# Waits at the two ends of an attention stage, and the work around them

## The reference

```python
x = x + tanh(g_xattn[0]) * attention(layernorm(x), ctx, ctx, mask)    # scores of all 16 heads, softmax, V, W_o
y = layernorm(x)
logits = einsum('bsd,ed->bse', y, gate_w); affinity = softmax(logits)
gating, idx = top_k(transpose(affinity), 56)                          # 56 rows of a batch for each expert
h = silu(y[idx] @ w_gate) * (y[idx] @ w_up)
x = x + tanh(g_ffn[0]) * scatter_add(idx, gating * (h @ w_down))
```

## Time and profile before

| | |
|---|---|
| median of three runs | 1863.48 us (1860.78 to 1865.54) |
| the profiled execution | 1861.66 us, its span 1859.8 us |
| TensorE busy in the span | 1738.0 us (93%), mean granted clock 0.974 |
| DVE, ScalarE, GpSimd busy | 1044.9, 840.6 and 204.0 us |
| attention stage, first scores to barrier | from 301 to 871 us |
| expert stage, first product to end | from 892 us |

### The profile page before, as it was taken

How to read it: one execution, slowest core, us unless ns; L and a number is a source line. 1 busy time by engine, 2 the same in 40 slices (tenths; PEclk the granted TensorE clock), 3 DMA queues, 4 the chain that set the end, 5 groups by cost and what they waited for, 6 DMA issues and landing times.

```text
span 1859.8 us, 28459 instructions
## 1 busy us (share of the span) xinstructions
PE 1738.0 (93%) x10502; PEld 1542.7 (83%) x10502; DVE 1044.9 (56%) x1801; ACT 840.6 (45%) x1483; POOL 204.0 (11%) x287
## 2 busy tenths in 40 slices
PE   7999993999999999993899999999999999999995
PEld 6998992778777777761899999999999999999995
DVE  6666662878877877854453544535445354353541
ACT  3232321878777777860443433434334344343430
POOL 0000010202211220201000201102001020020101
PEclk9999996999999999996899999999999999999998
DMA  6545446467567656613333533434335353353421
GB/s 235 219 177 195 175 156 186 124 141 185 139 139 178 159 134 157 158 54 103 115 107 108 142 114 112 138 105 141 113 100 152 103 141 112 102 151 104 121 101 20
DMA packets 76190, 251.90 MB, mean 135 GB/s; under 512 B 10785, under 2 KB 10785, under 8 KB 74817
## 3 DMA queue, kind: packets, MB, share of 16 engines
q1 hardware_dynamic: 63968, 215.88, 37.9%
q0 software_dynamic: 12128, 34.80, 8.1%
HBM read 188.01 MB, written 51.61 MB: 129 GB/s over the span
## 4 chain that ended last, share of the span: by engine, by line
PE 51%; POOL 1%; DMA 0%; DVE 0%; issue 0%; DVEq 0%; ACT 0%; POOLq 0%
PE gu_ps L1579 11%; PE gu_ps L1577 11%; PE gu_ps L1578 11%; PE y_ps L1594 6%; PE y_ps L1596 5%; PE y_ps L1595 5%; PE y_ps L1605 1%; PE gu_ps L1563 1%; DMA xg<-xn_rows,gather_i 0%; POOL out L1437 0%; POOL xg L1427 0%; DVE xs_lo L1512 0%; DVE y_cols L1539 0%; PE gu_ps L1623 0%; DVE y_sb L1517 0%
## 5 line engine op out<-in xcount | busy, mean ns | idle before, releaser
L1577 PE MATMUL gu_ps<-xs_hi,ws_hi 128*128 128x448 f32 x1024 | 371.7, 363 | 3.0 <-DVE xs_lo L1512 3.0
L1579 PE MATMUL gu_ps<-xs_hi,ws_lo 128*128 128x448 f32 x1024 | 371.8, 363 | 0.0
L1578 PE MATMUL gu_ps<-xs_lo,ws_hi 128*128 128x448 f32 x1024 | 370.5, 362 | 0.0
L1507 DVE TENSOR_TENSOR ws_lo<-w_raw,ws_hi 128x1024 fp32r<-128x1024 f32 x192 | 235.3, 1226 | 188.9 <-ACT ws_hi L1457 188.5
L1457 ACT ACTIVATE ws_hi<-w_raw 128x1024 fp32r<-128x1024 f32 x192 | 201.7, 1051 | 164.1 <-PE y_ps L1596 146.6
L1254 PEld LDWEIGHTS t_ps<-cst,sm 112*125 112x125 f32 x1536 | 204.3, 190 | 85.2 <-issue 32.4
L1254 PE MATMUL t_ps<-cst,sm 112*125 112x112 f32 x1536 | 234.0, 281 | 31.0 <-DVE e_t L978 14.3
L863 ACT ACTIVATE sm<-sm,least 112x752 f32<-112x752 f32 x256 | 234.4, 917 | 27.7 <-DMA v_rows<-v_out 16.8
L970 DVE CUSTOM_DVE_ANT_0 sm<-m_ps,mq 112x752 f32<-112x752 f32 x256 | 229.8, 935 | 29.8 <-PE m_ps L1238 28.1
L1577 PEld LDWEIGHTS gu_ps<-xs_hi,ws_hi 128*128 128x128 f32 x1024 | 192.3, 188 | 15.2 <-issue 3.3
L1578 PEld LDWEIGHTS gu_ps<-xs_lo,ws_hi 128*128 128x128 f32 x1024 | 192.3, 188 | 14.0
(11 more groups left out here) (146 smaller groups left out, 2408.4 us busy)
## 6 DMA issues: line engine op xcount, KB each, us to landing
w_raw<-wstream SPq DMA_DIRECT2D x192, 512.0 KB, 3.5
ks<-k_split SPq DMA_DIRECT2D x192, 188.0 KB, 5.4
k_split<-k_split SPq DMA_DIRECT2D x32, 752.0 KB, 3.4
v_rows<-v_out SPq DMA_DIRECT2D x16, 750.0 KB
vs<-v_rows SPq DMA_DIRECT2D x16, 750.0 KB
c_raw<-ctxT SPq DMA_DIRECT2D x7, 1500.0 KB, 12.8
qs<-q_hi POOLq DMA_DIRECT2D x64, 112.0 KB, 5.3
mq_raw<-maskq SPq DMA_DIRECT2D x7, 656.2 KB, 10.1
```

The source lines that it names most:

```text
L1507: nc.vector.tensor_tensor(w_lo[s][:], w_raw[s][:], w_hi[s][:], ALU.subtract).then_inc(wlo_done[s], 1)
L1577: nc.tensor.matmul(o, w_hi[s][:, w], xs_hi[:, c], start=(c == 0), stop=False)
L1578: nc.tensor.matmul(o, w_hi[s][:, w], xs_lo[:, c], start=False, stop=False)
L1579: mm = nc.tensor.matmul(o, w_lo[s][:, w], xs_hi[:, c], start=False, stop=(c == DC - 1))
```

## The change

It has four parts.

1. The mask of batch 0 is loaded by SyncE among the first loads, straight into mq, and masked in place by DVE after the norm of batch 0, early in the first stage; mq_first, GpSimd's waits for qs and its load are gone. In the attention stage SyncE waits only for the first store of each half of V before it loads V of batch 0. wo and gatew are loaded in turn 6 of batch 0, and TensorE waits for them where it first uses them. The eight tiles e_t are numbered anew, so that the three that overlay nothing (FREE_TILES) serve heads 0 to 2; ScalarE and DVE wait for all stores in turn 3 (early_stores), SyncE in turn 8.
2. x2_out goes from DVE's turn 10 to GpSimd's turn 12, ahead of the output store, which moved there from turn 9.
3. In the last batch the output projection is made in pieces (project_last) in m_ps[0] and m_ps[1], the score accumulators: two of the four quads after turns 14 and 15, the third before the last values, the fourth after. The turns of x2 (turn_last) take each half of the rows as soon as it is normed and go to w_ps and m_ps[1], copied by ScalarE and DVE. DVE's affinity of batch 6 stands before the last normalise.
4. w_raw lies where the keys of the attention stage lie, and SyncE loads the first four weight units in attend's end, once the last scores are made.

```diff
+            with ExitStack() as late:
+                sb(late, "below", [P, IC * SLOTS - E_OVER * (KC // 2) * PAIR])
+                w_raw = [sb(late, f"w_raw{j}", [P, UNIT]) for j in range(NRAW)]
             ks = sb(mid, "ks", [3 * WAYS, KSLOTS, SK], F32R)
-            with ExitStack() as early:
-                mq_first = sb(early, "mq_first", [QP, QC, S2], I32)
...
                 load_x(0)
+                sp.dma_start(mq[:, :, 0:S2].bitcast(I32), maskq[0:1].rearrange("o p c n -> p (o c) n")).then_inc(mq0_in, 16)
                 pair(0, False)
...
                                        part[g * DK:g * DK + DK].bitcast(F32)).then_inc(qs_in[g], 16)
-                for g in range(NG):
-                    hold(qs_in[g], 48)
-                pool.dma_start(both.mq_first[:], maskq[0:1].rearrange("o p c n -> p (o c) n")).then_inc(mq0_in, 16)
...
-                    nc.vector.tensor_scalar(mq[:, :, 0:S2], both.mq_first[:], 0, MASKED, ALU.is_equal, ALU.mult).then_inc(mq_done, 1)
+                    nc.vector.tensor_scalar(mq[:, :, 0:S2], mq[:, :, 0:S2].bitcast(I32), 0, MASKED, ALU.is_equal, ALU.mult).then_inc(mq_done, 1)
...
                 norm(0)
+                mask_queries()
                 with dve.Fori(1, B // 2 - 1) as i:
...
-        e_t = both.e_t + [sb(st, f"e_t{j}", [KP, KC // 2, PAIR]) for j in range(E_OVER, 2 * HG)]
+        e_t = [sb(st, f"e_t{j}", [KP, KC // 2, PAIR]) for j in range(E_OVER, 2 * HG)] + both.e_t
...
                 def start():
                     for k in range(KC // VT):
-                        hold(v_stored[k], 16 * B)
+                        hold(v_stored[k], 16)
                     load_v(0, 0)
-                    sp.dma_start(wo_sb[:], wo).then_inc(att_in, 16)
-                    sp.dma_start(gw_sb[:], gatew).then_inc(att_in, 16)
-                    for k in range(2):
-                        hold(k_stored[k], 16 * B * NG // 2)
...
+                        if t == 6 and first:
+                            sp.dma_start(wo_sb[:], wo).then_inc(att_in, 16)
+                            sp.dma_start(gw_sb[:], gatew).then_inc(att_in, 16)
+                        if t == 8 and first:
+                            for k in range(KC // VT):
+                                hold(v_stored[k], 16 * B)
+                            for k in range(2):
+                                hold(k_stored[k], 16 * B * NG // 2)
...

                 def end():
                     load_res(B - 1)
+                    hold(m_made, NS * B)
+                    for u in range(NRAW):
+                        sp.dma_start(w_raw[u][:], wstream[u]).then_inc(w_in[u], 16)
                     sp.wait_ge(x_in, 16 * (B + 1))
...
+                def x2_out(b, j):
+                    flag = flags_sb[:, j]
+                    hold(rest_free, R_USES * b + R_Y + 3)
+                    hold(flag_step, 5 * b + 5)
+                    hold(out_stored, 16 * b)
+                    for c in range(QC):
+                        nc.gpsimd.tensor_scalar(x2o[:, c], x2[:, c], flag[:, 3, c:c + 1], None, ALU.add).then_inc(x2o_done, 1)

                 def spread_parts(b, q):
...
+                            if t == 12:
+                                x2_out(b - 1, 1 - j)
                                 store_out(b - 1)
                         if not last:
...
-                def start():
+                def early_stores():
                     for k in range(KC // VT):
                         act.wait_ge(v_stored[k], 16 * B)
                     for k in range(2):
                         act.wait_ge(k_stored[k], 16 * B * NG // 2)
+
+                def start():
                     for h in range(XLEAD):
                         for qc in range(QC):
...
+                        if first and t == FREE_TILES:
+                            early_stores()
...
                     copy_parts(B - 1, NG - 1)
-                    for n in range(2):
-                        x2_columns(B - 1, n)
+                    x2_columns(B - 1, 0)
...
-                def x2_out(b, j):
+                def flags(b, j):
+
                     flag = flags_sb[:, j]
-                    dve.wait_ge(rest_free, R_USES * b + R_Y + 3)
-                    after(dve, out_stored, 16 * b)
-                    for c in range(QC):
-                        nc.vector.tensor_scalar(x2o[:, c], x2[:, c], flag[:, 3, c:c + 1], None, ALU.add).then_inc(x2o_done, 1)
-
-                def flags(b, j):
-
-                    flag = flags_sb[:, j]
+                    after(dve, x2o_done, QC * (b - 1))
                     for qc in range(QC):
                         dve.wait_ge(masked[qc], H * b + KSLOTS + 1)
...
-                def residual(b, c):
+                def residual(b, c, src):
...
-                            if t == 10:
-                                x2_out(b - 1, 1 - j)
                             if t == 15:
...
-                    for q in (NG - 2, NG - 1):
-                        normalise(b, q)
+                    normalise(b, NG - 2)
                     affinity(b - 1, (b - 1) % 2)
-                    residual(b, 0)
-                    residual(b, 1)
+                    normalise(b, NG - 1)
+                    for c in range(QC):
+                        residual(b, c, m_ps[c][0:QP, 0, :])
                     dve.wait_ge(rest_free, R_USES * b + R_Y + 3)
                     dve.nop(nofuse=True)
                     moments(b, 1, x2)
                     norm_2(b)
-                    x2_out(b, b % 2)
+                    dve.wait_ge(rest_made, R_USES * b + R_XNT + 2)
+                    nc.vector.tensor_copy(xT[:, 1], m_ps[1][:, 1, 0:2 * S]).then_inc(rest_free, 1)
...
+                            pe.wait_ge(att_in, 32)
...
+
+                def project_last(qc, quads):
+
+                    b = B - 1
+                    if quads[0] == 0:
+                        pe.wait_ge(masked[qc], H * B)
+                        pe.wait_ge(att_in, 32)
+                    pe.wait_ge(cx_done, NG * b + quads[-1] + 1)
+                    for q in quads:
+                        mm = nc.tensor.matmul(m_ps[qc][0:QP, 0, :], cx[:, q, qc * QP:qc * QP + QP], wo_sb[:, q, :],
+                                              start=(q == 0), stop=(q == NG - 1))
+                    if quads[-1] == NG - 1:
+                        mm.then_inc(rest_made, 1)
+
+                def turn_last():
+
+                    b = B - 1
+                    pe.wait_ge(rest_free, R_USES * b + R_XNT + 1)
+                    for qc in range(QC):
+                        pe.wait_ge(xn2_done, QC * b + qc + 1)
+                        for c in range(DC):
+                            a = c % 2 * S + qc * QP
+                            o = m_ps[1][:, 1, :] if c // 2 else w_ps
+                            mm = nc.tensor.transpose(o[:, a:a + QP], xn2[:, qc, c * P:c * P + P], ident[0:QP, 0:QP])
+                            if qc == QC - 1 and c % 2:
+                                mm.then_inc(rest_made, 1)

...
-                    pe.wait_ge(att_in, 32)
...
+                        if last and t >= H - QC:
+                            project_last(t - (H - QC), (0, 1))

                 def end():
                     b = B - 1
                     turn_parts(b, NG - 1)
+                    for qc in range(QC):
+                        project_last(qc, (2,))
                     for part in range(HG - 1):
                         values(b, NG - 1, part)
                     for qc in range(QC):
-                        for k in range(2):
-                            project_out(b, qc, k, True)
-                    for n in range(2):
-                        turn_x2(b, n)
+                        project_last(qc, (3,))
+                    turn_last()
                     logits(b)
                     turn_affinity()
...
-                for u in range(NU):
+                for u in range(NRAW, NU):
                     load(0, u)
```

29 lines of the change are left out of this document (16 added, 13 removed).

## The result

The changed kernel took **1838.74 us** in the median of four runs (1836.25 to 1839.79), the kernel before 1863.55 on the same chip (four runs, 1860.78 to 1865.54): a ratio of 0.9865, 95% interval 0.9853 to 0.9877, 24.8 us faster. Forecast were 42.0 us and a range of 1815 to 1834. The direction was right, the size was not: the time lies 4.7 us above the range.

A forecast was written before the change was run, and what follows sets the result against it. TensorE was taken to bound the kernel, gains lying only where it stands still: 29.0 + 4.6 + 3.4 + 1.5 + 3.5 = 42.0 us off 1861.7 gives 1819.7, as a median 1821.5; range 1815 to 1834.

The forecast's parts named there:

- Nothing in the change shortens a matmul, so all it can give lies where TensorE stands still: Whole kernel: gains only at the two seams of the attention stage and some tenths in each batch.
- Each is met by 0 to 5 us. I cost it at 0: First batch: stores at turn 3, V at turn 5 and K of head 8 arrive in time; cost 0.
- The rival of the late transfer: First batch: V, K of head 8 or the stores late, 3 to 11.5 us, typically 6, so 1827.5; chance 0.24.
- The first batch, 29.0 us: Seam from projections to first batch: waits for mask and gate weights go and the clock stays up; 29.0 us.
- I take it that 2.4 GHz stays: First seam: with scores after 1.5 us of silence the clock does not fall; 29.0 us in place of 26.2.
- the rival's 26.2: First seam: the clock falls all the same, 26.2 us in place of 29.0, so 1824.3; chance 0.18.
- x2_out, 4.6 us: Batches 1 to 7: x2_out leaves DVE's turn 10, saving 0.66 us a batch, seven times; 4.6 us.
- Both together are under 0.83, so both go: Steady batch: TensorE's waits of 0.47 and 0.19 us vanish as DVE loses 0.83 us of work.
- The lower bound of the term: Batches 1 to 7: x2_out's move gains 0 if ScalarE's copies take over.
- The gather, 3.5 us: First experts: gathers land 4.0 us after issue, with fewer weight loads beside them; 3.5 us, bounds 1.7 and 4.3.
- The splits can start with the stage: First experts: four weight loads done early, so splits start with the stage and three reloads meet the gather.
- The last batch, 3.4 and 1.5 us: Last batch: output projection in pieces gains 3.4 us; turns of x2 by halves bring the logits 1.5 us earlier.

The follow-up runs named there:

- 3: Changed kernel, but DVE waits before its first split of weights until GpSimd has copied the first expert's gather indices; 1840.29 us.
- 16: The kernel before with part 1 of the change alone, the moved waits and loads of the first batch; 1841.10 us.
- experiment 8: Changed kernel with three more transposes of a constant behind each of the first six scores, to keep TensorE busier; 1839.58 us.
- 10: Changed kernel, but DVE's first splits of the expert stage wait until the four gathers have landed; 1836.64 us.
- Experiment 9: Changed kernel with expert-stage tiles reordered: h_hi back at byte 99072, split weights moved, w_raw left where the change put it; 1831.32 us.
- experiment 1: Changed kernel with 64 bytes put ahead of h_hi and w_raw and 64 more ahead of xg, h_hi at byte 19968; 1849.28 us.
- experiment 6: Changed kernel, DVE's first splits to wait until the four gathers are issued, SyncE's loads of units 4 and on until they have landed; 1839.18 us.
- 5: Changed kernel with 64 bytes put ahead of h_hi and w_raw and 64 more ahead of the split weights, h_hi at byte 19968; 1836.49 us.
- 13: Changed kernel with h_hi at its old place, splits behind the gather, and batch 0's loads of mask, V, wo and gatew moved later; 1827.52 us.
- 15: The kernel before with part 2 of the change alone, x2_out on GpSimd in turn 12 ahead of the output store; 1859.70 us.
- 18: Kernel 13 run again, not altered; 1825.95 us.

## Why the prediction was wrong

- **The tile h_hi, not in the sum: 5.6 us.** The failed step is "Nothing in the change shortens a matmul, so all it can give lies where TensorE stands still": it took without a reason that nothing lengthens one either, and so put the expert stage at nothing. I read part 4 for its loads and did not price that it moves h_hi, the moving operand of 1024 of the 1536 matmuls of the second halves. The records of these halves came every 204 ns in place of 200. No row of the old trace could have given the price; the prediction should have said that it was unknown.
- **"Each is met by 0 to 5 us. I cost it at 0": measured 3.4 us in one profile, 6.4 in the other.** The rival of the late transfer was priced at 3 to 11.5, typically 6, and I gave it 0.24. Its price fits better than its mechanism: V, the stores and K of head 8, which it named, were in time in these two profiles (K of head 8 was late in 3 and 16), and the waits stand later, as far as batch 1. The backlog was worked out only as far as K of heads 8 and 9. The 16 KB of gatew, issued in turn 6, needed 24.6 us to land.
- **The first batch, 29.0 us: measured 26.3.** Both waits went, as priced. The failed step is "I take it that 2.4 GHz stays": the clock fell. From first score to first values that is 1.5 us (25.7 in place of 24.1); experiment 8 shows 0.9 of it. 1.0 us came by chance from the clock's first rise, and 0.2 from the barrier, behind which TensorE started 2.06 us after the last projection's start in place of 1.87. That the sum agrees with the rival's 26.2 is partly luck.
- **x2_out, 4.6 us: measured 2.3.** Both waits went, as the step "Both together are under 0.83, so both go" says. What failed is that nothing takes their place: ScalarE's copy did, with 0.5 to 0.6 us. The lower bound of the term named it. GpSimd's two instructions took 3.13 us, outside my 1.3 to 2.6 (the rows give 1.6 to 2.6), which cost nothing.
- **The gather, 3.5 us: measured 1.5.** "The splits can start with the stage" was the failed step: they collided with the index copy, so that the last gather went out 3.2 us later. Its landing was shortened by 4.0 us, more than the 3.5 I priced. With the splits held back until the gather has landed, the whole gives 4.7 (10).
- **The last batch, 3.4 and 1.5 us: measured 3.3 and 1.3.** Right, step by step.

Experiment 9, the changed kernel without the slower second halves, took 1831.32 us, inside the range. The late transfers weigh about as much (3.4 and 6.4 us), but the range had room for them and none for this omission.

## What to carry to other kernels

A tile that moves in SBUF is an edit of every instruction that reads it: compare the mean ns of the untouched groups before and after, and try the old addresses when they differ. When a barrier's silence is cut out, the transfers that it had covered move into the work behind it; follow each queue until a full batch later, not only to the first use. Work that comes earlier also meets other work: the weights that were early stalled the gather that they were to help.

## What the runs showed of the hardware

- Matmul records of 128x448 columns came every 200 ns, or up to 204 ns, by where the tiles lie in a partition; in experiment 1, where both operands lie in the same 64-byte half of 128 bytes, the first halves took 1.5 us more in 78.4. The Trainium skill (SBUF — State Buffer, SBUF: two separate sides) says that TensorE's reads wait for no other engine. Whether these runs go against that, or TensorE's own two reads collide, they don't show.
- GpSimd's indirect DMA issues took 0.93 us, and 1.93 beside DVE's splits (experiment 6).
- The clock fell to 1.2 GHz in turn 8 of batch 0, behind TensorE's waits of 0.9 to 1.0 and 1.0 to 1.2 us for DVE, in twelve of seventeen profiles with the new seam and in one of three with the old. The same waits stand in the others, where the clock stayed, so they don't decide it alone. The fall cost 1.2 to 2.0 us where nothing else was late (5, 13, 15, 18).
